# Layer 0's query, key and probability pairs are turned by DMA transposes instead of TensorE

## What is computed

```python
h = ada_rms(x, time_emb, ln1_w, ln1_tw)
q = (h @ Wq.T).reshape(b, s, NQ, HD).transpose(0, 2, 1, 3)    # NQ = 8, HD = 64
k = (h @ Wk.T).reshape(b, s, NKV, HD).transpose(0, 2, 1, 3)   # NKV = 1
v = (h @ Wv.T).reshape(b, s, NKV, HD).transpose(0, 2, 1, 3)
q = apply_rope(q, pos_ids)
k = apply_rope(k, pos_ids)
scores = jnp.einsum('bkgsd,bktd->bkgst', qg, k) / jnp.sqrt(jnp.float32(HD))
attn = jax.nn.softmax(scores, axis=-1)
ctx = jnp.einsum('bkgst,bktd->bkgsd', attn, v)
x = res + ctx @ Wo.T
h = ada_rms(x, time_emb, ln2_w, ln2_tw)
mlp = jax.nn.silu(h @ Wg.T) * (h @ Wu.T) @ Wd.T               # 512 -> 2048 -> 512
return res + mlp
```

## Time and profile before

| | us |
|---|---|
| median of 3 runs | 2566.2 (2564.31 to 2566.88) |
| profiled execution, its own time | 2565.41 |
| its span in the trace | 2563.5 |
| PE busy in the span | 2502.4 (98%) |
| DVE / ACT / POOL busy | 1392.8 / 960.8 / 1065.0 |
| first MLP matmul of layer 0 starts at | 120.02 |
| DMA packets' time, share of 16 engines | 16.7% |

### The profile page before, as it was taken

How to read it: one execution, slowest core, us unless ns; L and a number is a source line. 1 busy time by engine, 2 the same in 40 slices (tenths; PEclk the granted TensorE clock), 3 DMA queues, 4 the chain that set the end, 5 groups by cost and what they waited for, 6 DMA issues and landing times.

```text
span 2563.5 us, 47440 instructions
## 1 busy us (share of the span) xinstructions
PE 2502.4 (98%) x18502; PEld 1261.3 (49%) x18502; DVE 1392.8 (54%) x2150; ACT 960.8 (37%) x1560; POOL 1065.0 (42%) x1007
## 2 busy tenths in 40 slices
PE   7799999999999999999999999999999999999999
PEld 5445444454444544445454445554545455454544
DVE  7574343443434434344486575766757576775752
ACT  4352232322323223232343452635445262634542
POOL 3342222322223222232354455655556465654632
PEclk8999999999999999999999999999999999999999
DMA  6420101001010010100322412121121212111110
GB/s 220 170 73 18 39 3 49 8 17 40 3 50 7 17 39 3 50 7 15 120 83 82 129 31 77 28 60 43 52 67 30 80 26 72 43 51 55 30 63 29
DMA packets 113115, 133.30 MB, mean 52 GB/s; under 512 B 44686, under 2 KB 56078, under 8 KB 112916
## 3 DMA queue, kind: packets, MB, share of 16 engines
q1 hardware_dynamic: 112916, 130.26, 16.7%
HBM read 75.83 MB, written 18.74 MB: 37 GB/s over the span
## 4 chain that ended last, share of the span: by engine, by line
PE 85%; DVE 4%; POOL 4%; issue 3%; ACT 2%; DMA 1%; SPq 0%; POOLq 0%; DVEq 0%; ACTq 0%
PE ps_m L1588 47%; PE ps_abef L1588 19%; PE ps_d L1588 2%; PE ps_c L1588 2%; PE ps_abef L1797 2%; PE ps_abef L1790 2%; PE ps_abef L1792 2%; PE ps_abef L1826 1%; PE ps_d L1776 1%; PE ps_c L1642 1%; PE ps_abef L1834 1%; POOL inner L932 1%; PE ps_abef L1815 1%; POOL scratch L960 1%; PE ps_d L1689 1%
## 5 line engine op out<-in xcount | busy, mean ns | idle before, releaser
L1588 PE MATMUL ps_m<-h_mlp,weights 128*128 128x512 f16 x3168 | 726.8, 381 | 11.5 <-issue 5.0
L1588 PE MATMUL ps_m<-weights,inner 128*128 128x512 f16 x3072 | 693.8, 379 | 2.1 <-DVE scratch L1421 2.1
L1588 PEld LDWEIGHTS ps_m<-h_mlp,weights 128*128 128x128 f16 x3168 | 305.0, 98 | 360.3 <-issue 14.6
L932 POOL TENSOR_TENSOR inner<-scratch,inner 128x512 f16<-128x512 f32 x256 | 314.0, 1227 | 393.0 <-ACT inner L1117 392.8
L1588 PEld LDWEIGHTS ps_m<-weights,inner 128*128 128x128 f16 x3072 | 296.0, 98 | 336.1 <-issue 4.0
L1588 PE MATMUL ps_abef<-h_mlp,weights 128*128 128x512 f16 x1440 | 332.2, 379 | 0.0
L1117 ACT CAST inner<-scratch 128x512 f16<-128x512 f32 x256 | 157.0, 613 | 154.3 <-DVE scratch L1421 84.7
L1588 PEld LDWEIGHTS ps_abef<-h_mlp,weights 128*128 128x128 f16 x1440 | 136.5, 98 | 156.1 <-issue 4.2
L910 POOL TENSOR_TENSOR h_mlp<-scratch,h_mlp 128x512 f16<-128x512 f32 x64 | 74.0, 1156 | 191.4 <-ACT h_mlp L1072 191.4
L972 POOL TENSOR_TENSOR scratch<-scratch 128x512 f32<-128x512 f32 x64 | 72.6, 1134 | 163.3 <-DVE scratch L1475 163.3
L1072 ACT CAST h_mlp<-scratch 128x512 f16<-128x512 f32 x64 | 39.5, 618 | 262.3 <-POOL scratch L972 141.8
(11 more groups left out here) (173 smaller groups left out, 3673.2 us busy)
## 6 DMA issues: line engine op xcount, KB each, us to landing
x_mlp<-x_attn SPq DMA_DIRECT2D x64, 256.0 KB, 2.3
scratch<-scratch SPq DMA_DIRECT2D x128, 128.0 KB, 2.7
weights<-gamma SPq DMA_DIRECT2D x128, 128.0 KB, 2.9
x_attn<-x SPq DMA_DIRECT2D x32, 256.0 KB, 2.7
x_mid<-x_mlp SPq DMA_DIRECT2D x32, 256.0 KB, 2.3
x_attn<-x_mid SPq DMA_DIRECT2D x32, 256.0 KB, 2.7
out<-x_mlp SPq DMA_DIRECT2D x32, 256.0 KB, 2.2
inner<-wada_t SPq DMA_DIRECT2D x4, 1024.0 KB, 8.5
```

Of the source, the lines that this page charges most:

```text
L932: nc.gpsimd.tensor_tensor(inner[:, 1, j, :], src, inner[:, 0, j, :], ALU.subtract).then_inc(L.m_lo, 1)
L1588: ins = nc.tensor.matmul(o, left(a, k), right(b, k), start=(first and n == 0), stop=(last and n == len(order) - 1), skip_group_check=True)
```

## The change

Four things are done.

1. `turn` and `turn_p` leave PE. The query and key pairs now lie side by side in one buffer (`qkk0`, 1280 float16 columns), and SP turns them with one SBUF-to-SBUF DMA with `transpose=True` into `qkf0`; a second DMA turns the 1024 columns of probability pairs into `pt0`. The copies out of PSUM (`feature_major`, `key_major`) fall away with their steps. A DMA adds 16 to the semaphores `qf` and `pt`, and those who wait for them wait for multiples of 16.
2. The turned queries lie in another order (head, then token). `scores` becomes 32 matmuls in place of 16, each with the 64 tokens of one sequence and head as stationary columns, 64 moving columns, and one half of the output partitions. `mix` keeps eight matmuls and reads `pt0` with other steps.
3. The tables of due times are new: `CHAIN0`, `CHAIN0F`, the starts, the MLP's lags and the three set-up lists.
4. The two stores of layer 0's gains get a semaphore of their own (`first_gains_stored`), and the first `tanh` of the MLP waits for these two and no longer for all eight modulation stores.

```diff
+        qkk0 = carve(640).bitcast(F16)
+        qk0 = qkk0[:, 0:1024].rearrange("p (g h d) -> p g h d", g=HEADS0, h=2)
+        kk0 = qkk0[:, 1024:1280].rearrange("p (h r d) -> p h r d", h=2, r=2)
+        qkf0 = carve(640).bitcast(F16).rearrange("p (g n) -> p g n", g=10)
+        qf0, kf0 = qkf0[:, 0:8], qkf0[:, 8:10]
...
+                if stage == "turn":
+                    cut_done, scored = counts(tile(it, t) + 1, tile(it, t))
+                    sp.wait_ge(s_cond, 1)
+                    sp.wait_ge(L0.q_lo, cut_done)
+                    sp.wait_ge(L0.kk, cut_done)
+                    sp.wait_ge(L0.scores, scored)
+                    sp.dma_start(qkf0, qkk0, transpose=True).then_inc(L0.qf, 16)
+                if stage == "turn_p":
+                    cut_done, mixed = counts(tile(it, t) + 1, tile(it, t))
+                    sp.wait_ge(s_cond, 1)
+                    sp.wait_ge(L0.p_lo, cut_done)
+                    sp.wait_ge(L0.mixed, mixed)
+                    sp.dma_start(pt0, p0.rearrange("p g h t -> p (g h t)"), transpose=True).then_inc(L0.pt, 16)
...
-                if stage == "feature_major":
-                    nc.scalar.copy(kf0, as16(ps_pq[:, 0:128], 2)).then_inc(L0.kf, 1)
-                if stage == "key_major":
-                    nc.scalar.copy(pt0, as16(ps_d[:], 8)).then_inc(L0.pt, 1)
...
                         if first_block(it) and a == 0:
-                            act.wait_ge(s_ada_st, 16 * len(ADAS))
+                            act.wait_ge(s_gain_st, 16 * 2)
...
-                if stage == "feature_major":
-                    nc.vector.tensor_copy(qf0.rearrange("p b g q -> p g b q"),
-                                          as16(ps_c[:], 8).rearrange("p g (b q) -> p g b q", b=2)).then_inc(L0.qf, 1)
...
-                if stage == "turn":
-                    for g in range(HEADS0):
-                        nc.tensor.transpose(as16(ps_c[:], 8)[:, g, :], qk0[:, g].rearrange("p h d -> p (h d)"), ident16[:])
-                    for h in range(2):
-                        ins = nc.tensor.transpose(as16(ps_pq[:, 0:128], 2)[:, h, :], kk0[:, h].rearrange("p r d -> p (r d)"), ident16[:])
                 if stage == "scores":
-                    pe.wait_ge(L0.qf, n + 1)
-                    for b in range(2):
-                        for hp in range(4):
-                            for h in range(2):
-                                ins = nc.tensor.matmul(ps_d[:, (4 * b + hp) * SEQ:(4 * b + hp + 1) * SEQ],
-                                                       qf0[:, b, 2 * hp:2 * hp + 2, :].rearrange("p g q -> p (g q)"),
-                                                       kf0[:, h, SEQ * b:SEQ * (b + 1)], start=(h == 0), stop=(h == 1))
+                    pe.wait_ge(L0.qf, 16 * (n + 1))
+                    for g in range(HEADS0):
+                        for h in range(2):
+                            for b in range(2):
+                                tokens = slice(SEQ * b, SEQ * (b + 1))
+                                ins = nc.tensor.matmul(ps_d[tokens, SEQ * g:SEQ * (g + 1)], qf0[:, g, tokens],
+                                                       kf0[:, h, tokens], start=(h == 0), stop=(h == 1))
-                if stage == "turn_p":
-                    for g in range(8):
-                        ins = nc.tensor.transpose(as16(ps_d[:], 8)[:, g, :], p0[:, g].rearrange("p h t -> p (h t)"), ident16[:])
```

More of the change, by code:

```diff
@@ L134, in last_on @@
     return kind, sum(1 for s, t in seen if s in alike)
-NORM0 = list(zip(["stat", "rstd", "scale", "turn_x", "gain", "hi", "lo"], [0.0, -0.0, 0.1, 2.8, 3.6, 2.8, 6.3]))
+NORM0 = list(zip(["stat", "rstd", "scale", "turn_x", "gain", "hi", "lo"], [0, -0.2, 2.6, 3.8, 5.8, 7.5, 8.3]))
 CHAIN0 = [(s + "1", at) for s, at in NORM0] + [
-    ("proj", 7.7), ("rot", 12.3), ("qk_hi", 13.0), ("spread", 15.0), ("feature_major", 15.7), ("qk_lo", 17.0),
-    ("turn", 18.1), ("shift", 19.3), ("scores", 19.7), ("exp", 22.7), ("p_hi", 22.7), ("soft", 23.1), ("p_lo", 23.2),
-    ("turn_p", 29.9), ("c_lo", 29.9), ("key_major", 30.3), ("c_hi", 30.9), ("mix", 32.5), ("out", 35.3), ("add", 37.9)]
@@ L142 @@
[L142 removed]
+    ("proj", 7.5), ("spread", 8.1), ("qk_hi", 12.8), ("rot", 14.9), ("qk_lo", 17.0), ("turn", 17.9), ("scores", 21.5),
+    ("exp", 22.1), ("shift", 23.0), ("p_lo", 24.7), ("soft", 24.9), ("p_hi", 25.8), ("turn_p", 32.2), ("mix", 33.1),
+    ("c_hi", 34.5), ("out", 35.3), ("c_lo", 35.9), ("add", 37.8)]
+NORM0F = list(zip([s for s, _ in NORM0], [0, -0.1, -1.1, 1.1, 1.2, 6.0, 5.8]))
 CHAIN0F = [(s + "1", at) for s, at in NORM0F] + [
[L144 to L146 removed]
@@ new lines @@
+    ("proj", 2.5), ("rot", 7.4), ("turn", 9.0), ("qk_hi", 13.4), ("qk_lo", 13.7), ("spread", 17.7), ("scores", 18.0),
+    ("shift", 18.0), ("turn_p", 19.0), ("soft", 20.7), ("p_lo", 23.0), ("exp", 24.0), ("p_hi", 26.0), ("mix", 27.1),
+    ("c_lo", 30.9), ("c_hi", 31.9), ("out", 36.2), ("add", 37.9)]
+PE_COST0 = {"turn_x1": 0.45, "turn_x2": 0.45, "proj": 3.3, "scores": 0.5, "mix": 0.9, "out": 2.6}
+LAGS0 = {"up": [("tanh", 1.2), ("gated", 2.2), ("m_hi", 4.2), ("m_lo", 5.0)],
+         "down": [("y", 3.0), ("store", 3.6)]}
@@ L507, in __init__ @@
                 if n == 0:
+                    self.rot = s("rotated")
                     self.qk32 = s("qk32_ready")
```

90 lines of the change are left out of this document (31 added, 59 removed), and 6 rows, old and new, of the table SETUP_START0.

## The result

The changed kernel takes **2540.2 us** (median of 4 runs, 2537.6 to 2541.8) against 2566.5 us before: 0.990 times the time, 95% interval 0.9888 to 0.9912, 26.3 us less. Its profiled execution has a span of 2537.9 us, against 2563.5. The forecast was 15 us less; 2540.2 lies inside its range of 2534 to 2605, and the gain is close to twice what its sum gave (14.8).

What follows compares the result with a forecast made beforehand. PE's own time bounds layer 0's steady part: 1.01 us leaves and 0.48 is added a tile, 0.53 net, times 28 gives 14.8 us. Span 2548.7 plus 1.9 outside, 2551 us as median; range 2534 to 2605.

Steps and rivals of the forecast that it cites:

- What bounds: Layer 0's steady part: only PE's own time counts, busy 199.90 of 200 us; work taken off other engines gains nothing.
- What leaves PE: turn (0.56 us) and turn_p (0.45 us) leave PE: 1.01 us a tile, 28.3 us over 28 tiles.
- What is added: scores as 32 matmuls of 30 ns: 0.95 us in place of 0.47, so 0.48 us more a tile.
- The lower bound of the prediction: scores: the 16 ns a matmul hide, so 32 x 13.5 ns = 0.43 us, no more than before.
- The DMA's time: Each transposing DMA on SP lands 3.5 us after issue; low bound 2.3, high bound 12 (10 for the probabilities).
- the fixed 1.8 us of the sum: DMA transposes: landing time of small 16 KB DMAs, added to 1.3 us of packets to give 3.1 us.
- The windows: Ready input to needed output: 5.3 us for turn, 5.2 for turn_p; beyond cover each us costs 1 us.
- Set-up: Stretch before the first MLP matmul: taken as 0 change, between -5 and +6 us.
- the set-up grows: Rival: set-up transposes wait behind 1 MB strips, three by 5 us each, adding 15 us, 2566; chance 0.07.
- Layer 1: Layer 1 has the same code before and after and was given no gain.
- Semaphore: The first gains' own semaphore loosens one wait and can't cost; nothing was added for it.

Runs made afterwards that it cites:

- e5: The changed kernel with turn_p back on PE in the 28 steady tiles only, order of all other steps kept: 2556.1 us.
- e6: The changed kernel with turn and turn_p both back on PE in the 28 steady tiles only, order of all other steps kept: 2586.9 us.
- e4: The changed kernel with the loops of scores turned round, all matmuls of one output half before the other half: 2553.3 us.
- e7: The changed kernel with each DMA transpose done twice in series: 2655.5 us.
- e8: The changed kernel with scores placed earlier by 12 MLP matmuls in the steady table: 2569.5 us.
- e9: The changed kernel with the set-up's tables of the kernel before, two entries moved, and the new transposes: 2591.9 us.
- the other pair: Traces of e11 and of the changed kernel with one set-up transpose issued ahead of a strip (2539.9 us), the nearest repeats of both kernels.
- e11: The kernel before with only the separate semaphore for the first two stores of gains: 2566.2 us.
- e3: The changed kernel with the 32 matmuls of scores issued twice over in each tile: 2554.3 us.
- e12: The kernel before with forty idle matmuls on PE between the set-up and the first block: 2568.5 us.

## Why the prediction was right, point by point

- **What bounds.** Right. PE is still busy for 199.95 of 200 us from 600 to 800, as in the earlier trace rows; e5 shows that a turn given back costs nearly its instructions (15.9 us where they are 12.6, 2.5 of the rest being waits for ScalarE).
- **What leaves PE.** 1.01 us a tile, and e6's period has 4.0 us for four tiles. Right.
- **What is added: the step that was mis-sized.** The sum scaled `mix` and took 16 ns of every matmul as a fixed cost on top of the columns. `scores` takes 0.63 us and not 0.95. About 0.09 us more is hidden ahead of it: the 15 MLP matmuls before it should end at 527.25 at 0.216 each, and it starts at 527.34, a gap that the old `scores` in the earlier trace rows does not have and that `mix` has in both kernels. So +0.25 us a tile in place of +0.48, a net of 0.76 and not 0.53: 21.3 us in 28 tiles, 6.5 more than the sum had. The lower bound of the prediction, 13.5 ns and nothing on top, was nearer: doubling them costs 16 ns each. That the halves overlap at such short lengths, the other half of the reasoning, is right (e4). The measured block is 2.7 us shorter (159.75 to 157.1), not 3.0, since waits of 0.3 us at the blocks' heads take some back. All of layer 0's blocks: 19.9 us, 1.4 less than 21.3. The changed kernel's waits of 1.4 us up to 1200 us explain little of it, since the kernel before has one of 1.1; the rest was not found.
- **The DMA's time.** 3.4 and 3.1 us against 3.5 taken. The packets of 256 bytes are as supposed, but that the number fits so well is in part luck. The 16 ns a packet of the earlier trace rows were 21, some 0.4 us more for ten blocks, and SP's issue is 1.23 to 1.35 us and not 0.6. The issue does not come on top: the engines start 1.15 us after the issue's start and end some 0.5 us ahead of the landing, and these two are about the fixed 1.8 us of the sum. The Trainium skill's 1309 ns for one 128 x 128 transpose ("VectorE: DVE Perf Modes", "The three transpose paths") is not what ten in one instruction cost: 0.34 us each. What the Trainium skill says in "Advanced Engine Details and Errata", "X-Bar Transpose (TRN2)", that they are as fast as plain DMAs, is nearer, yet 3.1 us for 256 KB is more than the copy's 2.3 of the earlier trace rows.
- **The windows.** 5.3 us for the first, as said; 4.7 for the second, not 5.2. VectorE's last step of `soft` takes 1.30 us there and took 0.69 before. It now runs beside a GpSimd step:

```profile
531.15 1.30 DVE L1405 TENSOR_TENSOR scratch<-scratch 128x512 f32<-128x512 f32 x1
```

```profile
530.74 1.16 POOL L947 TENSOR_TENSOR inner<-scratch,inner 128x512 f16<-128x512 f32 x1 [6.33 <-ACT inner L1124]
```

In the whole trace 21 of the 32 such steps lie beside a GpSimd step for 0.75 us and take 1.29 or 1.30, and the other 11 lie beside none and take 0.69. e7 and e8 confirm the price beyond the window. Counted from SP's issue, the window is 5.2 us for the first turn and 4.7 for the second.

- **Set-up.** 0 forecast; 0.5 us longer in this pair of traces and 3.3 shorter in the other, but not because nothing happened there. e9 shows a set-up 34 us longer when the transposes meet the old tables; the new ones earn that back. So the 0 is right for a reason that the prediction does not give. The prediction's rival "the set-up grows", 15 us, was right in its mechanism (the first tile's `mix` waits 9.1 us for a turn_p behind a strip) and too small without the new list; the argument against it, that strips are issued long before, does not hold in the old list.
- **Layer 1.** "I give it nothing" missed 6.2 us between these two traces, of which 3 are the loop's head, 1.5 the clock and 1.7 open, and 2.1 us in the other pair. No row of the profile ahead of the change could have given its sign.
- **Semaphore.** Nothing forecast, nothing in e11.

In sum: +6.5 on the scores' term, -1.4 in layer 0's blocks, -0.5 for the set-up and +6.2 in layer 1 make 14.8 into 25.6. The mechanism that was forecast holds for 19.9 of them; the other 6 or so came from places where the forecast had nothing, and went its way by luck.

## What to carry to other kernels

When an engine is the bound, moving a step to a queue is worth its instructions there, as long as the time from the input's readiness to the consumer's turn is wider than the time from issue to landing; past that it costs one for one or a little more. What a step waits behind on that queue must be planned anew: the same eight transposes came with a set-up of 120.55 or of 154.90 us, by the set-up's tables alone. And to measure a step's worth, keep the order of all other work, or the new order is what one measures.

## What was not expected of the hardware

- Short matmuls on alternating column halves cost 16 to 20 ns each, those on one half after another 32 ns (e3, e4; 64 stationary and 64 moving columns).
- A DMA transpose of ten 128 x 128 blocks of 2-byte values takes SP 1.35 us to issue and is landed 3.4 us after the issue's start; eight blocks 1.23 and 3.1 us; 21 ns of engine time a packet of 256 bytes, with all 16 engines busy for some 1.4 us.
- The same VectorE step on 128 x 512 float32 values took 0.69 us alone and 1.30 beside a GpSimd step.
- Where a loop's head stood in PE's program was worth 0.6 us a pass of layer 1's loop and 1.5 of layer 0's (e12): waits for nothing that the profile shows came and went with instructions that do no work. e6 has the like, of 1.9 to 2.5 us, where it was not tested.
